# Mixture-of-experts outputs scaled and accumulated in DRAM instead of gathered back, in a decoder layer on one core

## The chip, the cores and the metric

The kernel is one launch on one core of a Trainium2 chip. The metric is the device time of that core in microseconds (us), the median of several executions. The engines are TensorE (PE, with its weight loads as PEld), VectorE (DVE), ScalarE (ACT), GpSimd (POOL) and SyncE (SP, which only issues transfers here). Sixteen DMA engines carry the transfers.

## The reference, cut to what matters

The layer works on 16 sequences of 256 tokens with 256 features each, 4096 tokens in all. It has three sublayers, each followed by a residual sum and a layer norm: gated linear attention, cross attention, and a mixture of 8 experts of which every token uses two. Only the third is touched:

```
probs = softmax(xf @ router_w.T)                 # 4096 x 8
topv, topi = top_k(probs, 2)
probs = probs * mask(topi);  probs /= probs.sum(-1) + 1e-9
g = einsum('nd,edf->nef', xf, gate_w) + gate_b   # d 256, f 512
u = einsum('nd,edf->nef', xf, up_w) + up_b
expert_out = einsum('nef,efd->ned', silu(g) * u, down_w) + down_b
y = einsum('ne,ned->nd', probs, expert_out)
out = layernorm(xf + y)
```

## The kernel before, in words

`decoder_layer` runs five stages one after the other. Each engine has its own instruction list in a stage, the lists are ordered among each other by semaphores only, and a stage begins when all engines and its transfers are through with the one before.

1. `linear_attention` and 2. `cross_attention` work sequence by sequence. The second ends a sequence by storing its normalised rows twice (`store_x2`, lines 888 to 891): into the SBUF tile `x2_all`, and into the DRAM tensor `x2_rows`. Its SP list begins with the loads of the first rows (lines 893 and 894).

3. `route_tokens` picks two experts for each token, almost all of it in one chain of small DVE instructions that each wait for the last (`link`, line 1484). It leaves the gates, the place (`slots`) of each of a token's two copies in a list sorted by expert, the same place as column and row, and a table that tells which expert a tile of the list belongs to.

4. `run_experts` inverts the places by one-hot matmuls into `token`, the token of each place, and then works through 23 tiles of the sorted list: 16 big ones of 512 rows and 7 half ones of 256. Products are made in three matmuls of high and low parts. For a tile t the lists interleave neighbouring tiles by hand:
   - PE: `gate_up` of t for f = 0 and 1, `down` of t-1 (one group of 12 matmuls for each 128 rows, alternating between two PSUM tiles `ps_y`, each of which must have been read by `keep_y` before it is used again, line 1955), `turn_x` of t+1, then `gate_up` for f = 2 and 3.
   - DVE: `hidden` 0 and 1, `keep_y` of t-1 (line 1854: PSUM plus bias into `y_out`), `hid_low` 0 and 1 (line 1880), `tile_index` of t+2 (line 1865), `x_low` of t+1, `hidden` and `hid_low` 2 and 3, `dn_low`.
   - ACT: `gu_high` of t+1, `gates` 0 and 1, `hid_high` 0 and 1, `x_high`, `dn_high`, `gates` and `hid_high` 2 and 3.
   - POOL: `low_parts` of t+1 (line 1767: four subtractions of 128x512 that make `gu_lo`), then `gather_rows` of t+2 (line 1758: one indirect transfer of 128 rows for each block, 4 or 2).
   - SP: weights of t+2, the store of y of t-1 into `y_sorted` (line 1719, after a wait for `keep_y`), biases of t+1.

5. `combine` takes the 32 blocks of 128 tokens in 16 groups of two. POOL gathers each token's two rows of `y_sorted` by `slots` (line 2023, 64 indirect transfers). DVE adds both, each times its gate, to `x2_all` (lines 2046 and 2052), takes mean and variance (lines 2057, 2061) and normalises (line 2067); ACT makes the root of the variance (lines 2034, 2036); SP stores (line 2090).

What orders the work around the change is thus POOL's list in stages 4 and 5, DVE's in stage 5, and the waits on `y_kept` and `y_stored`.

## Time and profile before

| | |
|---|---|
| time, median of 3 executions | 1540.83 us (1540.05 to 1543.04) |
| the profiled execution, its own time | 1540.89 us |
| its span, first to last instruction | 1539.0 us |
| mean granted TensorE clock | 0.927 |
| PE busy | 1315.0 us, 85% |
| DVE busy | 873.6 us, 57% |
| ACT busy | 890.7 us, 58% |
| POOL busy | 726.5 us, 47% |
| HBM read, written | 83.93 MB, 28.26 MB |

The busy shares are averages over five stages that have different limits, so what the change is worth has to be read stage by stage. All times in the rows are counted from the start of the span. By them cross attention runs from 747 us to about 1001, the routing to 1037, the experts to 1437, and the final stage to the end.

### The profile page before, as it was taken

To read this page: it belongs to the slowest core of one execution; us is meant where nothing else is said; L and a number is where in the kernel's file an instruction comes from. 1 tells how busy PE (TensorE), PEld (TensorE's weight loads), DVE (VectorE), ACT (ScalarE), POOL (GpSimd) and SP (SyncE) were. 2 spreads that over 40 slices of the span, in tenths; PEclk is the share of its full clock that TensorE was granted. 3 is DMA by queue.
4 is the path that set the end of the run, shared out by engine and by line. 5 is a ranking of instruction groups with operands and counts; after the bars stand their busy time and mean duration, and the time that the engine had idled before them with its cause. 6 is when DMAs were issued, how large, how long until landed. Compare 5 with 4: busy or idle time off the path is not lost. (4 is left out here: it accounts for less than half of the span.)

```text
span 1539.0 us, 31104 instructions
## 1 busy us (share of the span) xinstructions
PE 1315.0 (85%) x10439; PEld 1110.6 (72%) x10439; DVE 873.6 (57%) x1806; ACT 890.7 (58%) x2018; POOL 726.5 (47%) x861
## 2 busy tenths in 40 slices
PE   5899999999999999999689999804999999998200
PEld 4788888888888888887467777604788888898200
DVE  3345554544455545445378888577555555567447
ACT  4677777777777777777327777600554555455101
POOL 2244444444444444445347777402555454555464
PEclk9999999999999999999789999955899999999655
DMA  3300000000000000001123433204354545455244
GB/s 130 77 16 22 29 29 29 23 29 15 28 22 29 29 24 27 29 9 36 45 64 95 108 106 107 92 1 131 115 181 146 157 154 166 161 179 155 88 121 133
DMA packets 127907, 120.61 MB, mean 78 GB/s; under 512 B 42498, under 2 KB 108650, under 8 KB 127786
## 3 DMA queue, kind: packets, MB, share of 16 engines
q1 hardware_dynamic: 120970, 100.42, 21.0%
q0 software_dynamic: 6816, 18.62, 4.6%
q8 instruction: 70, 1.15, 0.3%
q14 instruction: 51, 0.42, 0.1%
HBM read 83.93 MB, written 28.26 MB: 73 GB/s over the span
## 5 line engine op out<-in xcount | busy, mean ns | idle before, releaser
L293 POOL TENSOR_SCALAR_AFFINE_SELECT a_decay<-a_decay 128x256 f32<-128x256 f32 x256 | 115.3, 454 | 258.7 <-ACT a_decay L373 257.2
L496 DVE TENSOR_TENSOR a_probs<-a_ps_s,a_decay 128x384 f32<-128x384 f32 x256 | 131.6, 552 | 158.3 <-PE a_ps_o L676 147.4
L302 POOL TENSOR_TENSOR a_key_sum<-a_probs 128x256 f32<-128x256 f32 x128 | 94.5, 738 | 170.0 <-DVE a_probs L496 158.0
L336 ACT ACTIVATE a_qk_exp<-a_ps_qk 128x512 f32<-128x512 f32 x128 | 76.5, 598 | 136.9 <-PE a_ps_qk L582 130.0
L1767 POOL TENSOR_TENSOR e_gu_lo<-e_gu_raw,e_gu_hi 128x512 fp32r<-128x512 f32 x92 | 117.3, 1305 | 72.2 <-ACT e_gu_hi L1788 72.2
L582 PE MATMUL a_ps_qk<-a_xT_hi,a_w_hi 128*128 128x256 f32 x512 | 145.0, 283 | 3.6 <-ACT a_qk_relu L337 3.6
L582 PE MATMUL a_ps_qk<-a_xT_hi,a_w_lo 128*128 128x256 f32 x512 | 143.9, 281 | 0.0
L582 PE MATMUL a_ps_qk<-a_xT_lo,a_w_hi 128*128 128x256 f32 x512 | 143.8, 281 | 0.0
L489 DVE SCALAR_TENSOR_TENSOR a_qk<-a_qk_exp,a_qk_relu 128x512 f32<-128x512 f32 x128 | 89.2, 697 | 96.1 <-ACT a_qk_relu L337 96.0
L657 PE MATMUL a_ps_s<-a_qk 64*128 64x256 f32 (+1 forms) x1024 | 131.7, 337 | 0.7 <-DVE a_probs L496 0.5
L1758 POOL DMA_INDIRECT e_x_in<-x_rows,e_index x78 | 75.0, 961 | 115.6 <-DVE e_index L1865 98.5
L371 ACT ACTIVATE a_decay<-a_ps_c,a_c_now 128x256 f32<-128x256 f32 x256 | 124.4, 486 | 1.8 <-PE a_ps_c L647 1.2
L1816 ACT CAST e_hid_hi<-e_hid 128x512 fp32r<-128x512 f32 (+1 forms) x92 | 48.9, 554 | 128.0 <-PE e_ps_y L1958 87.5
L670 PE MATMUL a_ps_o<-a_probs,a_values 128*64 128x256 f32 (+1 forms) x1024 | 111.5, 339 | 0.4 <-DVE a_probs L496 0.4
L657 PEld LDWEIGHTS a_ps_s<-a_qk 64*128 64x128 f32 x1024 | 107.3, 186 | 2.5 <-issue 2.5
L582 PEld LDWEIGHTS a_ps_qk<-a_xT_hi,a_w_hi 128*128 128x128 f32 x512 | 98.0, 191 | 5.8 <-issue 5.6
L373 ACT ACTIVATE a_decay<-a_ps_c,a_c_now 128x128 f32<-128x128 f32 x256 | 98.4, 384 | 0.0
L582 PEld LDWEIGHTS a_ps_qk<-a_xT_hi,a_w_lo 128*128 128x128 f32 x512 | 98.1, 192 | 0.0
L582 PEld LDWEIGHTS a_ps_qk<-a_xT_lo,a_w_hi 128*128 128x128 f32 x512 | 97.9, 191 | 0.1
L307 POOL TENSOR_TENSOR a_oT_lo<-a_oT,a_oT_hi 128x256 fp32r<-128x256 f32 x128 | 94.4, 737 | 1.2 <-ACT a_oT_hi L390 1.2
L1874 DVE SCALAR_TENSOR_TENSOR e_hid<-e_ps_u,e_bias,e_gate 128x512 f32<-128x512 f32 (+1 forms) x92 | 61.0, 668 | 57.3 <-ACT e_gate L1810 45.7
L955 POOL TENSOR_TENSOR b_probs<-b_probs,b_top 128x1232 f32<-128x1232 f32 x32 | 72.7, 2272 | 43.3 <-DVE b_top L1132 43.3
(282 smaller groups left out, 4007.7 us busy)
## 6 DMA issues: line engine op xcount, KB each, us to landing
e_gu_raw<-in_L_ffn_gate_w SPq DMA_DIRECT2D x23, 512.0 KB
e_gu_raw<-in_L_ffn_up_w SPq DMA_DIRECT2D x23, 512.0 KB
e_dn_raw<-in_L_ffn_down_w SPq DMA_DIRECT2D x23, 512.0 KB, 4.4
y_sorted<-e_y_out SPq DMA_DIRECT2D x16, 512.0 KB
a_x_in<-in_x SPq DMA_DIRECT2D x16, 256.0 KB, 2.8
a_x_res<-in_x SPq DMA_DIRECT2D x16, 256.0 KB, 2.8
x_rows<-a_x SPq DMA_DIRECT2D x16, 256.0 KB, 2.1
x_bo_rows<-a_x_bo SPq DMA_DIRECT2D x16, 256.0 KB, 2.1
```

Source lines behind the costliest of these rows:

```text
L293: pool.affine_select(out=d, in_=d, compare_op=ALU.is_ge, fill=0.0, base=0, pattern=[[0, 2], [1, P]], channel_multiplier=-1)\
L302: pool.tensor_tensor(key_sum[:], probs[:, :, P:N], probs[:, :, N:TRI], ALU.add).then_inc(keys_summed, 1)
L307: pool.tensor_tensor(oT_lo[g % 2][:], oT[g % 2][:], oT_hi[g % 2][:].bitcast(F32), ALU.subtract).then_inc(oT_lo_done, 1)
L336: act.activation(qk_exp[:], ps_qk[:], ACT.Exp)
L371: act.activation(decay[h][:, 0:N], ps_c[:, h, :], ACT.Exp, bias=c_now[:, 0, head:head + 1], scale=-1.0)
L373: act.activation(decay[h][:, N:TRI], ps_c[:, h, P:N], ACT.Exp, bias=c_now[:, 1, head:head + 1], scale=-1.0).then_inc(decay_exp[h], 1)
L489: vec.scalar_tensor_tensor(qk[g][:], qk_exp[:], 1.0, qk_relu[:], ALU.min, ALU.add).then_inc(qk_done, 1)
L496: vec.tensor_tensor(probs[:, h, :], ps_s[h][:, 0:TRI], decay[h][:], ALU.mult)\
L582: mm = pe.matmul(out, l, r, start=(n == 0), stop=(n == len(todo) - 1))
L657: mm = pe.matmul(ps_s[h][:, out], qk[g][rows, 1, j], qk[g][rows, 0, i], start=True, stop=True)
L670: pe.matmul(out[h][:, 0, cols], values[par][:, j, 2 * g + h, :], probs[:, h, keys], start=(j == 0), stop=(j == 1), skip_group_check=True)
L1767: ins = pool.tensor_tensor(gu_lo[par][:, k, cols], gu_raw[par][:, k, cols], gu_hi[par][:, k, cols].bitcast(F32), ALU.subtract)
```

## The change

- A token's rows in DRAM get four more columns (`META`), written by the routing: the difference of the two gates, the second gate, the number of the first expert, the first gate. The gather of a tile brings them along, and DVE works out from them each row's `share`, the gate that belongs to this tile's expert.
- ACT multiplies the rows of `y_out` by their share. POOL adds them by indirect accumulating transfers to the tokens' rows of a new DRAM tensor `sum_rows`, in which cross attention has put the rows themselves. Those of tile t are issued when the ones of tile t-1 have landed.
- Places that no token uses get targets of their own (`spare`, 512 more rows, zeroed at the start of cross attention).
- `x2_all`, `slots`, `y_sorted` and the store of y are gone. The final stage loads `sum_rows` in order, in 8 groups of four blocks, and shares out the normalising: two blocks to ACT, one to DVE, one to POOL.

```diff
 def cross_attention(...):
+        spare = sb("b_spare", [P, D + META])
             def store_x2(b):
                 sp.wait_ge(x2_ready, b + 1)
-                sp.dma_start(x2_all[:, bass.ts(b, NB), :], x2[:]).then_inc(x2_stored, 16)
+                sp.dma_start(sum_rows[b], x2[:]).then_inc(x2_stored, 16)
                 sp.dma_start(x2_rows[b], x2[:]).then_inc(x2_stored, 16)
 
+            sp.wait_ge(spare_ready, 1)
+            for n in range(B * N, x2_dram.shape[0], P):
+                sp.dma_start(x2_dram[n:n + P, :], spare[:]).then_inc(spare_stored, 16)
+                sp.dma_start(sum_dram[n:n + P, :], spare[:, 0:D]).then_inc(spare_stored, 16)
             sp.dma_start(x_in[:], x1_rows[0]).then_inc(x_in_loaded, 16)
...
         def _(pool):
+            pool.memset(spare[:], 0.0).then_inc(spare_ready, 1)
...
 def route_tokens(...):
+        @block.sync
+        def _(sp):
+            sp.wait_ge(meta_ready, 1)
+            sp.dma_start(x2_dram[0:plan.TOKENS, D:D + META].rearrange("(n p) m -> p n m", p=P), meta[:]).then_inc(meta_stored, 16)
+            sp.wait_ge(meta_stored, 16)
...
                 if k == 0:
+                    link(vec.tensor_scalar(meta[:, :, 2], col[:], -1.0, float(E), ALU.mult, ALU.add))
...
                 link(vec.tensor_tensor(gates[k][:], top[k][:], rcol[:], ALU.mult))
+            link(vec.tensor_tensor(meta[:, :, 0], gates[0][:], gates[1][:], ALU.subtract))
+            link(vec.tensor_copy(meta[:, :, 3], gates[0][:]))
+            vec.tensor_copy(meta[:, :, 1], gates[1][:]).then_inc(meta_ready, 1)
...
-                vec.tensor_copy(slots[k][:], slot_f[:]).then_inc(slots_ready, 1)
-                vec.wait_ge(slots_ready, k + 1)
...
 def run_experts(...):
-            def load_biases(e, par):
+            def load_biases(e, t, par):
+                if has(t, -2):
+                    for n in range(2):
+                        sp.wait_ge(y_kept[n], rounds(t - 1))
...
-                if has(t, -1):
-                    store(t - 1, 1 - par)
...
+            pool.iota(spare_i[:], pattern=[[0, -(-COLS // TB)], [P, TB]], base=plan.TOKENS + 1, channel_multiplier=1).then_inc(counts_ready, 1)
...
+            def add_rows(t, par, turn):
+                pool.wait_ge(y_scaled, first_block(t + 1))
+                pool.wait_ge(target_ready, t + 1)
+                if has(t, -1):
+                    pool.wait_ge(y_stored[1 - par], 16 * plan.blocks_of_parity(t - 1, turn - 1 + par))
+                pool.sem_inc(pool_turns, 1)
+                for blk in range(blocks(t)):
+                    pool.indirect_dma_start(sum_dram, bass.IndirectOffsetOnAxis(target[par][:, blk:blk + 1], 0),
+                                            y_out[par][:, blk, :], None, compute_op=ALU.add).then_inc(y_stored[par], 16)
+
             def tile(t, par, turn):
                 if has(t, 1):
                     low_parts(1 - par, turn + par)
+                if has(t, -1):
+                    add_rows(t - 1, 1 - par, turn - 1 + par)
                 if has(t, 2):
                     gather_rows(t + 2, par, turn + 1)
...
+                def scale_y(blk):
+                    act.wait_ge(y_kept[blk % 2], rounds(t - 1) + blk // 2 + 1)
+                    act.activation(y_out[1 - par][:, blk, :], y_out[1 - par][:, blk, :], ACT.Copy,
+                                   scale=share[1 - par][:, blk:blk + 1]).then_inc(y_scaled, 1)
+
                 gates(0)
                 gates(1)
+                if has(t, -1):
+                    act.wait_ge(share_ready, t)
+                    for blk in range(blocks(t - 1) - 1):
+                        scale_y(blk)
                 hid_high(0)
                 hid_high(1)
+                if has(t, -1):
+                    scale_y(blocks(t - 1) - 1)
...
             def keep_y(t, par, turn):
-                vec.wait_ge(y_stored[par], 16 * turn)
+                if has(t, -2):
+                    vec.wait_ge(y_stored[par], 16 * plan.blocks_of_parity(t - 2, turn - 1))
+                vec.tensor_copy(target[par][:, 0:blocks(t)], token[:, bass.ds(first_block(t), blocks(t))]).then_inc(target_ready, 1)
...
+            def shares(t, par):
+                if has(t, -2):
+                    vec.wait_ge(y_scaled, first_block(t - 1))
+                nb = blocks(t)
+                vec.scalar_tensor_tensor(share[par][:, 0:nb], x_in[par][:, 0:nb, D + 2], expert_of[:, bass.ds(t, 1)],
+                                         x_in[par][:, 0:nb, D], ALU.is_equal, ALU.mult).then_inc(share_step, 1)
+                vec.wait_ge(share_step, t + 1)
+                vec.tensor_tensor(share[par][:, 0:nb], share[par][:, 0:nb], x_in[par][:, 0:nb, D + 1], ALU.add).then_inc(share_ready, 1)
...
                     x_low(t + 1, 1 - par)
+                    shares(t + 1, 1 - par)
...
-            vec.tensor_copy(token[:], ps_u[0][:, 0:COLS]).then_inc(token_kept, 1)
+            vec.scalar_tensor_tensor(used[:], ps_u[0][:, 0:COLS], 0.0, spare[:, 0:COLS], ALU.is_equal, ALU.mult).then_inc(token_kept, 1)
             vec.wait_ge(token_kept, 1)
+            vec.scalar_tensor_tensor(token[:], ps_u[0][:, 0:COLS], -1.0, used[:], ALU.add, ALU.add).then_inc(token_kept, 1)
...
 def combine(...):
-    G = 2
-    BUFS = 4
+    G = 4
+    ON_ACT = (0, 1)
+    ON_VEC, ON_POOL = 2, 3
...
+            for i in range(GROUPS):
+                sp.dma_start(rows[i][:], sum_rows[:, cols(i), :]).then_inc(loaded[i], 16)
+            for i in range(GROUPS):
+                sp.wait_ge(act_done, i + 1)
+                sp.wait_ge(vec_done, i + 1)
+                sp.wait_ge(pool_done, i + 1)
+                sp.dma_start(out_rows[:, cols(i), :], rows[i][:]).then_inc(stored, 16)
...
+            def statistics(i):
+                vec.wait_ge(loaded[i], 16)
+                for j in range(G):
+                    vec.bn_stats(stats[:, i * G + j, :], rows[i][:, j, :]).then_inc(counted, 1)
+                vec.wait_ge(counted, G * (i + 1))
+                vec.sem_inc(vec_turns, 1)
+                for j in range(G):
+                    ins = vec.bn_aggr(mv[:, i * G + j, :], stats[:, i * G + j, :])
+                ins.then_inc(var_ready, 1)
+
+            def normalise(i):
+                vec.wait_ge(rstd_ready, i + 1)
+                vec.scalar_tensor_tensor(shift[:, cols(i)], mv[:, cols(i), 0], -1.0, rstd[:, cols(i)], ALU.mult, ALU.mult)\
+                    .then_inc(shift_ready, 1)
+                n = i * G + ON_VEC
+                vec.tensor_scalar(rows[i][:, ON_VEC, :], rows[i][:, ON_VEC, :], mv[:, n, 0:1], rstd[:, n:n + 1],
+                                  ALU.subtract, ALU.mult).then_inc(vec_done, 1)
```

In the new final stage DVE and ACT each do the first step of group i and then the normalising of group i-1, and POOL normalises its block of group i.

## Rows read from the trace of the kernel before

**Rows 1.** Windows: stretch, length, PE PEld DVE ACT POOL busy (count), PEclk, DMA share, GB/s.

```profile
1200.00:1240.00 40.00, 40.00 (x235) 35.14 (x234) 23.02 (x36) 21.08 (x29) 20.21 (x19) 1.00 0.56 174
...
1437.00:1539.00 102.00, 0.00 (x0) 0.00 (x0) 56.21 (x160) 9.28 (x33) 62.26 (x65) 0.51 0.41 124
...
1049.00:1051.00 2.00, 0.17 (x1) 0.02 (x1) 2.00 (x3) 1.04 (x1) 2.00 (x2) 0.50 1.01 374
```

**Rows 2.** Groups by line, 1430 to 1539: count, busy us, mean ns, idle before, releaser.

```profile
L2023 POOL DMA_INDIRECT f_y<-y_sorted,slots x64 | 62.2, 971 | 25.9 <-issue 19.2 <-DVE f_stats L2057 6.7
...
L2057 DVE BATCH_NORM_STATS2 f_stats<-f_resid 128x6 f32<-128x256 f32 x32 | 12.0, 419 | 3.0 <-DVE f_resid L2052 2.6
L2067 DVE TENSOR_SCALAR f_resid<-f_resid,f_mv,f_rstd 128x256 f32<-128x256 f32 x32 | 11.8, 410 | 0.0
L2034 ACT ACTIVATE f_ln_var<-f_mv,f_eps_col 128x2 f32<-128x2 f32 x16 | 4.7, 296 | 88.3 <-DVE f_mv L2061 54.0 <-issue 21.6 <-remote 12.8
L2061 DVE BATCH_NORM_AGGREGATE f_mv<-f_stats 128x2 f32<-128x6 f32 x32 | 4.0, 166 | 4.3 <-issue 1.7 <-DVE f_stats L2057 1.7
```

**Rows 3.** Chain that ended last, final stage: start, length, what.

```profile
1457.51 2.63 DMA f_y<-y_sorted,slots
```

**Rows 4.** Timeline, both ends of the final stage: start, length, engine, line, operation, idle before.

```profile
1434.34 0.43 DVE L1854 TENSOR_TENSOR e_y_out<-e_ps_y,e_dn_bias 128x256 f32<-128x256 f32 x1 [2.07 <-PE e_ps_y L1958]
...
1437.35 0.10 POOL L2015 MEMSET f_eps_col<- 128x1 f32 x1 [19.55 <-POOLq L1617]
...
1534.77 1.42 DVE L2067 TENSOR_SCALAR f_resid<-f_resid,f_mv,f_rstd 128x256 f32<-128x256 f32 x4
```

**Rows 5.** Page, part 6, transfers: count, KB each, median us to landing.

```profile
e_dn_raw<-in_L_ffn_down_w SPq DMA_DIRECT2D x23, 512.0 KB, 4.4
...
a_x_in<-in_x SPq DMA_DIRECT2D x16, 256.0 KB, 2.8
```

**Rows 6.** Timeline of a big tile, 1220 to 1239: POOL, then ACT, then DVE.

```profile
1221.05 5.05 POOL L1767 TENSOR_TENSOR e_gu_lo<-e_gu_raw,e_gu_hi 128x512 fp32r<-128x512 f32 x4 [2.87 <-ACT e_gu_hi L1788]
1230.79 0.97 POOL L1758 DMA_INDIRECT e_x_in<-x_rows,e_index  x1 [4.69 <-DVE e_index L1865]
...
1238.37 5.07 POOL L1767 TENSOR_TENSOR e_gu_lo<-e_gu_raw,e_gu_hi 128x512 fp32r<-128x512 f32 x4 [2.86 <-ACT e_gu_hi L1788]
...
1227.95 1.15 ACT L1816 CAST e_hid_hi<-e_hid 128x512 fp32r<-128x512 f32 x2 [4.83 <-PE e_ps_y L1958]
...
1223.82 0.42 DVE L1854 TENSOR_TENSOR e_y_out<-e_ps_y,e_dn_bias 128x256 f32<-128x256 f32 x1
...
1228.61 1.29 DVE L1880 TENSOR_TENSOR e_hid_lo<-e_hid,e_hid_hi 128x512 fp32r<-128x512 f32 x2 [0.29 <-ACT e_hid_hi L1816]
1229.82 0.16 DVE L1865 CAST e_index<-e_token 128x4 uint32 x1
```

**Rows 7.** Timeline of a half tile, 1370 to 1382: POOL, then DVE.

```profile
1370.91 5.23 POOL L1767 TENSOR_TENSOR e_gu_lo<-e_gu_raw,e_gu_hi 128x512 fp32r<-128x512 f32 x4 [2.56 <-ACT e_gu_hi L1788]
...
1381.32 5.24 POOL L1767 TENSOR_TENSOR e_gu_lo<-e_gu_raw,e_gu_hi 128x512 fp32r<-128x512 f32 x4 [1.79 <-ACT e_gu_hi L1788]
...
1373.62 2.81 DVE L1880 TENSOR_TENSOR e_hid_lo<-e_hid,e_hid_hi 128x256 fp32r<-128x256 f32 x2
```

**Rows 8.** Timeline, start of the experts: DVE without and with POOL's subtractions beside it.

```profile
1045.26 1.93 DVE L1911 TENSOR_SCALAR e_col_hot<-e_count,slot_col,e_number 128x78 fp32r<-128x78 f32 x8
...
1048.24 5.85 DVE L1911 TENSOR_SCALAR e_col_hot<-e_count,slot_col,e_number 128x78 fp32r<-128x78 f32 x8
...
1048.88 4.93 POOL L1767 TENSOR_TENSOR e_gu_lo<-e_gu_raw,e_gu_hi 128x512 fp32r<-128x512 f32 x4 [11.11 <-ACT e_gu_hi L1788]
```

**Rows 9.** Timeline of cross attention: its start (SP, PE), and ACT's normalising near its end.

```profile
747.37 0.38 SPq L893 DMA_DIRECT2D b_x_in<-x_rows  x1
...
753.08 1.09 PE L1237 MATMUL b_ps_m<-ident,b_x_in 128*128 128x128 f32 x4 [0.24 <-ACT b_rwT L987]
...
996.34 1.09 ACT L1041 ACTIVATE b_x<-b_resid,b_shift,b_rstd 128x256 f32<-128x256 f32 x2
```

More of the change, by code:

```diff
@@ L16 @@
 LN_EPS = 1e-5
+META = 4
 class Shapes:
@@ L1837, in _ @@
             all_tiles(act, tile)
+            last = TILES - 1
+            act.wait_ge(share_ready, TILES)
+            for blk in range(blocks(last)):
+                act.wait_ge(y_kept[blk % 2], rounds(last) + blk // 2 + 1)
+                act.activation(y_out[last % 2][:, blk, :], y_out[last % 2][:, blk, :], ACT.Copy,
+                               scale=share[last % 2][:, blk:blk + 1]).then_inc(y_scaled, 1)
         @block.vector
@@ L1919, in _ @@
             x_low(0, 0)
+            shares(0, 0)
             dn_low(0, 0)
@@ L2005, in combine @@
[L2005 to L2009 removed]
+        rows = [sb(f"f_rows{i}", [P, G, D]) for i in range(GROUPS)]
+        stats, mv = sb("f_stats", [P, NBK, 6]), sb("f_mv", [P, NBK, 2])
@@ new lines, in _ @@
+        @block.vector
+        def _(vec):
+            def statistics(i):
[14 more added lines that the diff above has]
+                                  ALU.subtract, ALU.mult).then_inc(vec_done, 1)
+            for i in range(GROUPS):
+                statistics(i)
+                if i:
+                    normalise(i - 1)
+            normalise(GROUPS - 1)
@@ L2085, in _ @@
[L2085 to L2092 removed]
+                n = i * G + ON_POOL
+                pool.wait_ge(rstd_ready, i + 1)
```

183 lines of the change are left out of this document (71 added, 112 removed).

## The prediction

> **What bounds the kernel now.** I read the windows by stage first, then the groups by line of the final stage and its chain, then the timelines of one big and one half tile. In a window of big tiles PE is busy all 40.00 us of 40, at the full clock, POOL half of them, the DMA engines 0.56 [rows 1]: PE bounds the big tiles, and what is added to other engines there is free until it makes PE wait. In the final stage PE does nothing, and POOL is the busiest with 62.26 of 102 us [rows 1]. Its 64 gathers take 62.2 us, with 25.9 us of idle time before them, 19.2 of it the gaps of 0.3 us between two issues [rows 2]; the chain goes gather, landing (2.63 us from an issue), DVE [rows 3]. So the stage is set by one gather after the other at 0.97 + 0.30 = 1.27 us, 81 us in all, and the rest is DVE's sums. It runs from 1437.35 to 1539.0 [rows 4], 101.7 us, 6.6% of the span. This is what the change can win.
>
> **The final stage, after.** No gathers; 8 loads and 8 stores of 512 KB. DVE has for each group four statistics at 12.0/32 = 0.375 us (1.50), four aggregates at 4.0/32 = 0.125 (0.50), one block normalised at 11.8/32 = 0.37, all [rows 2], a small operation for the shift (0.2, the nearest is the index copy of 0.16 [rows 6]) and two waits on its own semaphores, 0.1 each: 2.8 us, 22.4 for eight. ACT has a root (two operations of at most 0.30 [rows 2]) and two blocks of 1.09 together [rows 9], 1.7 us a group, less than DVE. The first load lands in 4.4 us [rows 5]. Behind the last statistics come root 0.6, shift 0.2, ACT's blocks 1.1, waits 0.3 and a store of 4.4, less the 0.6 of DVE's own last step that is counted already. Sum: 4.4 + 22.4 + 6.0 = 32.8, say 33 us.
>
> The transfers are the unknown. 512 KB land 1.6 us later than 256 KB [rows 5], which by itself would mean 3.2 us for each further 512 KB, and 4.4 + 15 x 3.2 = 52 us for loads and stores in a row. With the DMA engines full, 374 GB/s are moved [rows 1], 1.4 us for 512 KB, 22 us for all 16. Eight loads queued at once are the second case, so I take the 33 of DVE. Bounds 30 and 52. The term is 33 - 101.7 = **-68.7 us** (-72 to -50).
>
> **The seam before it.** Now y is kept at 1434.77 and the stage begins at 1437.35 [rows 4]. After: ACT's scaling 0.6, POOL's lead before a run of indirect transfers 0.8 (the index copy ends at 1229.98, the gather starts at 1230.79 [rows 6]), a second issue 1.27 later, landing 2.63 [rows 3]: 1440.1. An accumulating transfer is not in this trace; its landing is bounded by that of a gather from below and, with no row near, by twice that from above; I add 0.4. **+3 us** (2.5 to 6).
>
> **Big tiles.** A tile is 1238.37 - 1221.05 = 17.3 us [rows 6]. POOL's list becomes subtraction, adds, gathers: 5.05 + 0.2, then twice a lead of 0.8 and 5.0 for four issues = 16.9 us. That fits by 0.4. In time: ACT is through with `hid_high` at 1229.1 [rows 6], the last scaling at 1229.6 (0.5, half of the 1.09 [rows 9]; the three before it lie in ACT's 4.83 us of idle time [rows 6]), adds 1230.4 to 1235.4, gathers 1236.2 to 1241.2. The subtraction that began at 1238.37 now runs from 1241.3 to 1246.4; PE needs it only in the next tile. The 0.5 us on ACT before `x_high`, the two `shares` operations and the target copy on DVE have slack in the tile, since PE is fed two halves ahead. One thing I don't take as free. The target copy stands in front of `keep_y`, which starts at 1223.82, one period later 1241.15, next to the new start of the subtraction. Of what DVE does beside a subtraction the trace shows this: eight `col_hot` operations take 1.93 us, and 5.85 us with a subtraction beside them [rows 8]; two `hid_low` take 2.81 us beside one in a half tile [rows 7] and 1.29 us for twice the columns without [rows 6]. Each seems to wait for one of the four subtractions, 5.05/4 = 1.26 us. A copy held so long delays the reading of a PSUM tile that PE wants back one group of 12 matmuls later, 2 us or less by 235 matmuls in 40 us [rows 1], of which reading itself needs 0.42 [rows 6]. So between 0 and 1.3 us for each of 15 tiles; I take 0.33. **+5 us** (0 to 19).
>
> The Trainium skill says in "SBUF — State Buffer", section "Who interferes with whom", that copies and casts in a two-port mode share a port pair with GpSimd, and that the one issued second is blocked until the other is through. The rows on `col_hot` agree; that a copy of four elements is held too, no row here shows. By the rule alone the term would be that of the rival below.
>
> **Half tiles.** The period is 1381.32 - 1370.91 = 10.4 us [rows 7], already a loop of POOL's 5.2 us and the DVE work that waits for its end. POOL's list becomes 5.24 + 0.2 + 2 x (0.8 + 0.97 + 0.3 + 0.95) = 11.5 us, 1.1 more, in the five half tiles that have all three jobs; and `shares` adds 0.4 us to the loop of DVE. The larger counts: **+5 us** (0 to 10).
>
> **Small edits.** Cross attention: SP must wait for POOL's memset (0.3) and issue eight spare stores at 0.4 each before the first load, which now goes at 747.37 [rows 9]; it goes at about 751.2 and lands in 2.8 us [rows 5] or a little more behind 1 MB of stores: 754.5, where PE wanted it at 753.08 [rows 9]. **+1.5 us** (0 to 4). `x2_all` becomes a store to DRAM, with the same count of issues at the same places of SP's list; nothing. Routing: four small DVE operations in, two out; three of the new ones fall where DVE waits for PE; nothing. The store of 16-byte pieces has the rest of the routing, some 24 us from the gates to its end, as cover; without it, it would delay the first gather. Start of the experts: three small DVE operations more, **+0.6**. SP loses 23 stores and keeps the same waits before the biases. The new wait of the adds is for those of the tile before, issued 17 us (10 in half tiles) earlier; behind it stand POOL's gathers and subtraction, and it stays empty unless four adds take that long.
>
> **The sum**: -68.7 + 3 + 5 + 5 + 1.5 + 0.6 = -53.6, a span of 1485.4. The profiled execution took 1540.89 for a span of 1539.0, 1.9 more, and lies 0.06 above the median; so the median is 1487.
>
> **Rivals.**
> - *Issuing an add costs more than a gather.* With I for an issue and its gap, each 1 us above 1.27 costs 4 us in a big tile, less the 0.4 of slack, and 2 in a half one: 74 (I - 1.27) - 6 on top, and less for small ones. At one and a half times (0.97 becomes 1.45) that is 29 us, 1516. For: it writes by address to DRAM and must read as well. Against: all 64 gathers stay close to 0.97, whatever else goes on. Chance 0.12.
> - *The same, and slower than before.* The place is POOL's list in the experts. It decides from I = 1.27 + 60/74 = 2.1 us; at 3 us the time would be 1487 + 122 = 1609. The same is reached where the four adds of a tile take over 17.3 + 3.4 us to land, 5 us each, against 2.63 for a gather. Chance 0.06. "Collectives: The Full Stack" of the Trainium skill, section "The bandwidth ceiling", says that an add in the DMA engines needs two reads where a copy needs one and runs at half its rate; no row here shows one. That would be 128 KB more in each, far from 5 us, and it leaves the chance small.
> - *The target copy always waits for a whole subtraction.* 15 x 1.3 instead of 5: 1501. For: the new start of the subtraction and the copy fall together. Against: the subtraction may fall just behind, and PE has about a microsecond of slack. Chance 0.10.
> - *The final stage is bounded by transfers*, 52 us for 33: 1506. Chance 0.08.
> - *All additions hide*: without the two terms of 5 and the 1.5, 1475. Chance 0.04. That the change doesn't do what it says can't be more than part of this: 64 gathers leave the final stage in any case.
> - The forecast: 0.60, own range 1479 to 1495.
>
> **Range and chances.** 1476 to 1517 leaves out the slower case, the best one, and half of the dear issue, some 0.16 to 0.2. A difference of 0.2% (3 us) is about what can be told from none. Faster by more: all but the slower case and what lies beside it, 0.93; the same 0.01; slower 0.06.
>
> **What would show it.** The final stage should be 30 to 36 us with DVE busy nearly throughout and no wait for a load after the first; if DVE waits for loads, that term is wrong. The group of adds on POOL should show 0.95 to 1.0 us each; if 1.4 or more, the first rival. PE should stay at 40 of 40 in big tiles, at a period of 17.3 to 17.7; if PE waits on DVE's `keep_y` there, the copy is held. The half tiles should have a period near 11.4 and POOL with hardly a gap. The first PE work on x in cross attention should come 1 to 2 us late. A chain that goes through the landing of adds before the last tile would prove me wrong altogether.

## The result, and the profile after

The changed kernel takes 1508.97 us (1504.07 to 1511.16, four runs) beside 1541.30 (1540.05 to 1543.04) for the kernel before: a ratio of 0.9777, with a 95% interval of 0.976 to 0.9793. The forecast was 1487, the range 1476 to 1517. So the direction and the range held, and of the 54 us that were expected about 32 came.

The profiled execution took 1509.18 us for a span of 1507.5, against 1539.0 before. I cut both spans at the same two events on VectorE: the first operation of the experts' stage (the copy that makes `e_count`) and the start of the last kept y rows. The times are starts in the timelines.

| stretch, us | before | after | difference | forecast |
|---|---|---|---|---|
| to the start of the experts | 1037.8 | 1040.7 | +2.9 | +1.5 |
| from there to the first tile index of the loop | 54.2 | 54.4 | +0.2 | +0.6 |
| 14 periods of big tiles | 241.8 | 250.5 | +8.7 | +5 |
| last big one and the half tiles, six periods | 73.8 | 94.4 | +20.6 | +5, with the next line |
| to the last kept y | 26.8 | 29.9 | +3.2 | |
| seam and final stage | 104.7 | 37.6 | -67.1 | -65.7 |

The end came out as forecast; the loss is in the middle, above all in the half tiles. First the windows, with the columns of [rows 1]:

```profile
1200.00:1240.00 40.00, 39.95 (x228) 34.66 (x227) 28.11 (x45) 24.27 (x38) 34.88 (x28) 1.00 0.59 142
1360.00:1400.00 40.00, 31.99 (x210) 30.12 (x211) 19.96 (x45) 20.55 (x39) 28.25 (x22) 0.88 0.55 130
1400.00:1440.00 40.00, 34.00 (x248) 33.53 (x246) 26.91 (x51) 23.16 (x44) 31.00 (x25) 0.87 0.59 166
1480.00:1507.00 27.00, 0.00 (x0) 0.00 (x0) 16.75 (x80) 12.95 (x33) 9.88 (x8) 0.50 0.89 312
```

In the big tiles PE still looks fully busy, 39.95 of 40 [rows 1]. It is not as productive: 228 matmuls in the window against 235. A busy share near its limit hides a period that has grown from 17.33 to 17.86 us. POOL went from 20.21 to 34.88 busy, and with the gaps of 0.3 us between issues that is all of its time. In the half tiles PE is down to 32 and 34 of 40, and its granted clock to 0.88 and 0.87. In the kernel before, the clock of the window from 1360 to 1400 was 1.00.

Why POOL is full, by its groups over the experts' stage (busy us, mean ns, idle time before and what ended it):

```profile
L1796 POOL DMA_INDIRECT sum_rows<-e_y_out,e_target x78 | 126.6, 1623 | 45.9 <-ACT e_y_out L1851 21.2 <-issue 19.9 <-ACT e_y_out L1884 4.5
L1785 POOL TENSOR_TENSOR e_gu_lo<-e_gu_raw,e_gu_hi 128x512 fp32r<-128x512 f32 x92 | 116.6, 1304 | 20.2 <-ACT e_gu_hi L1819 19.9
L1776 POOL DMA_INDIRECT e_x_in<-x_rows,e_index x78 | 79.7, 1022 | 45.4 <-DVE e_index L1926 22.2 <-issue 21.9 <-DMA sum_rows<-e_y_out,e_target 0.9
```

An add takes POOL 1.62 us to issue, a gather 1.02 beside it and 0.97 in [rows 2]. I had costed the adds at the gather's price. The timeline of one big tile, POOL's list and then two operations of VectorE in the same tile (start, length):

```profile
1214.44 5.06 POOL L1785 TENSOR_TENSOR e_gu_lo<-e_gu_raw,e_gu_hi 128x512 fp32r<-128x512 f32 x4
1219.67 1.88 POOL L1796 DMA_INDIRECT sum_rows<-e_y_out,e_target  x1 [0.17 <-issue]
1221.86 1.56 POOL L1796 DMA_INDIRECT sum_rows<-e_y_out,e_target  x1 [0.30 <-issue]
...
1227.41 1.09 POOL L1776 DMA_INDIRECT e_x_in<-x_rows,e_index  x1 [0.30 <-issue]
...
1232.32 1.31 POOL L1785 TENSOR_TENSOR e_gu_lo<-e_gu_raw,e_gu_hi 128x512 fp32r<-128x512 f32 x1
...
1217.46 3.20 DVE L1941 TENSOR_TENSOR e_hid_lo<-e_hid,e_hid_hi 128x512 fp32r<-128x512 f32 x2 [0.28 <-ACT e_hid_hi L1847]
1220.59 0.42 DVE L1926 CAST e_index<-e_token 128x4 uint32 x1
```

No wait for another engine stands in POOL's list ("issue" is time in which it waited for nothing that the profile shows): it ends at 1232.3 and starts again at once, 17.88 us after 1214.44. Beside it two `hid_lo` take 3.20 us instead of 1.29 [rows 6]: VectorE's work has come to lie beside POOL's subtraction.

The half tiles open with a stall, in the last big tile. The timeline again, VectorE, POOL, TensorE:

```profile
1355.26 5.14 DVE L1900 CAST e_target<-e_token 128x4 uint32<-128x4 f32 x1
...
1355.43 4.94 POOL L1785 TENSOR_TENSOR e_gu_lo<-e_gu_raw,e_gu_hi 128x512 fp32r<-128x512 f32 x4
1368.69 1.62 POOL L1796 DMA_INDIRECT sum_rows<-e_y_out,e_target  x1 [8.33 <-ACT e_y_out L1851]
...
1376.17 1.00 POOL L1776 DMA_INDIRECT e_x_in<-x_rows,e_index  x1 [0.30 <-ACT e_gu_hi L1819]
...
1397.89 1.11 PE L2001 MATMUL e_ps_x<-ident,e_x_in 128*128 128x128 f32 x4 [6.15 <-DMA e_x_in<-x_rows,e_index]
```

A copy of four elements a row takes 5.14 us, to within 0.03 us of the end of POOL's subtraction. It comes to lie there because POOL's list has just become shorter: the first half tile has two gathers and not four, and so this subtraction begins 15.93 us after the one before it (1339.50) and not 17.86. The y rows behind the copy are kept late, so scaled late, so POOL waits 8.33 us before its adds, and the gathers stand behind the adds. What PE then waited for, from 1355 to 1470 (us, times, longest):

```profile
PE e_ps_x L2001 <- DMA e_x_in<-x_rows,e_index: 12.4, 4, 6.2
PE e_ps_g L2012 <- DVE e_hid L1935: 5.3, 4, 2.0
PE e_ps_y L2024 <- DVE e_y_out L1904: 4.1, 1, 4.1
PE e_ps_y L2024 <- DVE e_hid_lo L1941: 2.2, 1, 2.2
```

These waits are not the whole loss. The stretch from the start of the six periods to the last kept y, before and after, in the columns of [rows 1]; then two windows of the changed kernel in it:

```profile
1333.80:1434.34 100.54, 91.37 (x696) 86.81 (x694) 66.29 (x121) 53.39 (x98) 49.69 (x42) 0.99 0.50 154
1345.62:1469.91 124.29, 100.15 (x688) 95.23 (x687) 77.36 (x146) 62.69 (x117) 89.50 (x66) 0.90 0.52 125
1415.00:1420.00 5.00, 5.00 (x44) 5.00 (x44) 3.53 (x8) 3.41 (x6) 4.38 (x4) 1.00 0.88 236
1425.00:1430.00 5.00, 5.00 (x24) 5.00 (x25) 2.08 (x8) 2.38 (x5) 4.19 (x3) 0.50 0.56 137
```

PE sits idle 24.1 us instead of 9.2, which is 15.0 of the 23.8 us. The other 8.8 us are busy time: the same work takes 100.2 us instead of 91.4, and the granted clock of the stretch is 0.90 instead of 0.99. Between the two small windows PE was busy 0.55 of 5 us; behind that wait the clock stood at 0.50 of its full 2.4 GHz, and PE, busy all the time, started 24 matmuls where it had started 44. The matmuls of y follow each other every 0.21 us at 1361, at half the clock, and every 0.12 at 1211, at the full one.

The seam and the start of the final stage, then three pieces of the chain in one of its groups:

```profile
1470.37 0.51 ACT L1884 ACTIVATE e_y_out<-e_y_out,e_share 128x256 f32<-128x256 f32 x1 [0.87 <-DVE e_y_out L1904]
1471.70 1.54 POOL L1796 DMA_INDIRECT sum_rows<-e_y_out,e_target  x1 [4.54 <-ACT e_y_out L1884]
1473.55 1.54 POOL L1796 DMA_INDIRECT sum_rows<-e_y_out,e_target  x1 [0.30 <-issue]
1479.76 7.38 SPq L2083 DMA_DIRECT2D f_rows<-sum_rows  x8
```

```profile
1486.20 1.30 DVE f_stats L2096 x4
...
1487.63 0.38 DVE f_mv L2100 x4
...
1488.06 0.38 DVE f_rows L2108
```

The final stage runs from 1479.76 to 1507.5, 27.8 us where it took 101.7 [rows 4]. Its chain is VectorE's from the first load's landing at 1484.24 on: 2.21 us a group, with no wait for a load after the first.

### The profile page after: what moved, and what is told of

The parts are those of the page before. It is cut to its first block and busy times, and to the rows that moved or that the text cites. A ratio compares the mean times of both kernels' runs of the same rounds, so it can differ in the third digit from the quotient of the medians.

```text
span 1507.5 us, 31113 instructions
## 1 busy us (share of the span) xinstructions
PE 1331.5 (88%) x10439; PEld 1124.8 (75%) x10439; DVE 873.7 (58%) x1799; ACT 930.7 (62%) x2096; POOL 804.1 (53%) x885
## 3 DMA queue, kind: packets, MB, share of 16 engines
q0 software_dynamic: 14976, 20.62, 7.5%
## 5 line engine op out<-in xcount | busy, mean ns | idle before, releaser
L1796 POOL DMA_INDIRECT sum_rows<-e_y_out,e_target x78 | 126.6, 1623 | 45.9 <-ACT e_y_out L1851 21.2
L490 DVE SCALAR_TENSOR_TENSOR a_qk<-a_qk_exp,a_qk_relu 128x512 f32<-128x512 f32 x128 | 89.1, 696 | 94.5 <-ACT a_qk_relu L338 94.4
L1785 POOL TENSOR_TENSOR e_gu_lo<-e_gu_raw,e_gu_hi 128x512 fp32r<-128x512 f32 x92 | 116.6, 1304 | 20.2 <-ACT e_gu_hi L1819 19.9
L1941 DVE TENSOR_TENSOR e_hid_lo<-e_hid,e_hid_hi 128x512 fp32r<-128x512 f32 (+1 forms) x92 | 91.2, 1010 | 33.4 <-ACT e_hid_hi L1847 32.3
L1776 POOL DMA_INDIRECT e_x_in<-x_rows,e_index x78 | 79.7, 1022 | 45.4 <-DVE e_index L1926 22.2
L2024 PE MATMUL e_ps_y<-e_dn_hi,e_hid_hi 128*128 128x256 f32 x312 | 89.9, 288 | 6.7 <-DVE e_y_out L1904 4.5
## 6 DMA issues: line engine op xcount, KB each, us to landing
a_x_in<-in_x SPq DMA_DIRECT2D x16, 256.0 KB
a_x_res<-in_x SPq DMA_DIRECT2D x16, 256.0 KB, 2.7
x_rows<-a_x SPq DMA_DIRECT2D x16, 256.0 KB, 2.2
x_bo_rows<-a_x_bo SPq DMA_DIRECT2D x16, 256.0 KB, 2.2
b_x_in<-x_rows SPq DMA_DIRECT2D x16, 256.0 KB, 3.0
```

Source lines behind the costliest of these rows:

```text
L1785: ins = pool.tensor_tensor(gu_lo[par][:, k, cols], gu_raw[par][:, k, cols], gu_hi[par][:, k, cols].bitcast(F32), ALU.subtract)
L1796: pool.indirect_dma_start(sum_dram, bass.IndirectOffsetOnAxis(target[par][:, blk:blk + 1], 0), y_out[par][:, blk, :], None, compute_op=ALU ...
L1941: vec.tensor_tensor(hid_lo[:, f, 0:rows], hid[n][:, 0:rows], hid_hi[:, f, 0:rows].bitcast(F32), ALU.subtract)\
L2024: mm = pe.matmul(ps_y[n][:, 0:D], h[:, f, rows], w[par][:, f, :], start=(s == 0), stop=(s == len(todo) - 1))
```

## The experiments

Absolute times of different comparisons stand on different chips: the kernel before took 1541 and 1545 us on two of them and 1529 to 1531 on three others. I could not place that difference; its mean granted clock was 0.928 to 0.931 where it took 1529 to 1532 us and 0.923 to 0.929 where it took 1543 to 1548, and which of the two made the other is not shown. In the kernels after the change the stretches agree from chip to chip: last kept y to end takes 37.6 and 37.3 us in the changed kernel on two chips, and 36.8 and 37.0 in e7 and e9, again on two. So between comparisons I go by stretches of the traces, and use ratios to tell how each kernel stands to the one before.

| run | ratio to before | big tile, us | 14 periods | six periods | start of experts to last y | to the end |
|---|---|---|---|---|---|---|
| before | 1 | 17.33 | 241.8 | 73.8 | 396.5 | 104.7 |
| changed | 0.9777 | 17.86 | 250.5 | 94.4 | 429.2 | 37.6 |
| e1 | 1.0321 | 23.87 | 323.4 | 91.5 | 501.1 | 36.4 |
| e2 | 1.0061 | 20.2 | 279.5 | 92.5 | 459.0 | 37.5 |
| e3 | 0.9782 | 17.5, 17.8 | 248.1 | 86.7 | 418.8 | 37.0 |
| e4 | 0.9932 | 18.3 | 256.1 | 96.1 | 435.8 | 37.5 |
| e5 | 0.9774 | 17.8, 18.8 | 254.1 | 94.3 | 432.8 | 37.3 |
| e6 | 0.9732 | 18.3 | 256.0 | 84.7 | 421.9 | 36.8 |
| e7 | 0.9696 | 18.1 | 253.9 | 80.9 | 417.5 | 36.8 |
| e8 | 0.9825 | 18.1 to 21.4 | 270.5 | 86.8 | 439.2 | 36.0 |
| e9 | 0.9684 | 17.53 | 246.3 | 73.7 | 402.1 | 37.0 |
| e10 | 0.9645 | 17.53 | 246.3 | 73.7 | 401.9 | 35.3 |
| e11 | 0.9680 | 17.85 | 249.0 | 76.0 | 407.5 | 31.3 |
| e12 | 0.9638 | 17.53 | 246.3 | 73.7 | 400.4 | 35.5 |

e1 to e4 shared a chip, e5 to e8 another, e9 to e11 a third; e12 ran on a fourth.

### e1: scatter instead of add

```
-  y_out[par][:, blk, :], None, compute_op=ALU.add)
+  y_out[par][:, blk, :], None)
```

> The indirect transfers of the experts' rows write them instead of adding them (the sums lose the tokens' own rows and one of the two experts); waits, lists and sizes stay. Theory A (the price of an add's issue on POOL, 1.62 us in the trace after against 1.02 for a gather, makes POOL the bound of the experts' stage): the issue falls to about 1.0, POOL's list of a big tile from 17.9 to 15.5 us, the period of a big tile returns to 17.3 (-8 us over 14 tiles), the half tiles lose 1.2 us of POOL each (-8): about 1492, 1485 to 1498. Rival B (the accumulating packets, 72 us of 16 engines, crowd the gathers and loads): the issue stays near 1.6 and the time falls all the same, by 10 or more, while the packets get shorter. Rival D (1.6 us is the price of any indirect destination): issue stays at 1.6, packets shorter or not, time within 3 us of 1509.

It became slower, 1579.32 us, ratio 1.0321 (1.0304 to 1.0339), where the cheaper issue was to make it faster. The price itself came out as expected. POOL's group, then the two operations that explain the rest, from the timelines:

```profile
L1796 POOL DMA_INDIRECT sum_rows<-e_y_out,e_target x78 | 80.6, 1033 | 163.1 <-ACT e_y_out L1851 140.0
```

```profile
1218.84 4.96 POOL L1785 TENSOR_TENSOR e_gu_lo<-e_gu_raw,e_gu_hi 128x512 fp32r<-128x512 f32 x4
...
1219.45 4.38 DVE L1900 CAST e_target<-e_token 128x4 uint32 x1
```

An issue costs 1.03 us without the addition and 1.62 with it: 0.59 us is the addition's, not the scatter's, which rules out rival D. But POOL's shorter list moved the subtraction against VectorE's: the target copy now begins 0.61 us after the subtraction, as it does in most big tiles, and ends with it, at 1223.83 against 1223.80. The 23 copies take 73.9 us in all, against 10.0 in the changed kernel, and the period is 23.87. So a cheaper step made the kernel some 5% slower, by its phase. As a test of what the add's price costs it failed; e11 had to do that. Nor can it decide on rival B, since the held copies set its pace. The packets did change: the same 20.62 MB move in half of them and half the time, as the page's rows of the software queue show (packets, MB, share of 16 engines; the changed kernel, then e1). What speaks against rival B is e9, which has all 14,976 packets of the adds and yet a period of 17.53 us.

```profile
q0 software_dynamic: 14976, 20.62, 7.5%
```

```profile
q0 software_dynamic: 7488, 20.62, 3.8%
```

### e2: gathers ahead of adds

```
 if has(t, 1): low_parts(...)
+if has(t, 2): gather_rows(t + 2, ...)
 if has(t, -1): add_rows(t - 1, ...)
-if has(t, 2): gather_rows(t + 2, ...)
```

> On POOL the gather of tile t+2 is issued before the adds of tile t-1. Theory A: the list of a big tile keeps its length, 17.9 us; what goes is the stall in which the gathers of the half tiles stood behind adds that waited for the scaled rows and a landing (PE waited 12.4 us for x rows between 1360 and 1460): half tiles fall from 13.7 to 11 or 12 us; about 1492, 1484 to 1500. Rival E (POOL now waits for the index, which VectorE has only 8.8 us after the tile begins, with the adds behind it): idle of up to 3.8 us a big tile, period 18.5 to 21, time 1515 to 1560.

1539.34 us, ratio 1.0061 (1.0044 to 1.0077). Rival E's number held, 20.2 us a big tile, but not quite for its reason:

```profile
1207.48 5.59 POOL L1785 TENSOR_TENSOR e_gu_lo<-e_gu_raw,e_gu_hi 128x512 fp32r<-128x512 f32 x4
1215.20 1.01 POOL L1776 DMA_INDIRECT e_x_in<-x_rows,e_index  x1 [2.13 <-DVE e_index L1926]
...
1210.27 3.96 DVE L1941 TENSOR_TENSOR e_hid_lo<-e_hid,e_hid_hi 128x512 fp32r<-128x512 f32 x2 [0.28 <-ACT e_hid_hi L1847]
```

POOL waits 2.13 us for the index, and the index is late because it stands behind two `hid_lo` of 3.96 us (5.55 in the next tile) instead of 1.29, beside POOL's subtraction. The subtraction holds up the copy for which POOL then waits. The half tiles gained nothing: 92.5 for 94.4 in the six periods, and 2.5 us more from there to the last kept y. Theory A's 1492 failed.

### e3: half of the subtraction on VectorE

```
-for k in range(KC):      # POOL
+for k in range(1, KC):
+vec.tensor_tensor(gu_lo[par][:, 0, :], gu_raw[par][:, 0, :],
+                  gu_hi[par][:, 0, :]..., ALU.subtract)
```

> Half of the gate and up weights' subtraction (two of POOL's four of 1.30 us) goes to VectorE as one of 128x1024, about 1.1 us, while it waits for the turned rows. Theory A: POOL's list of a big tile is 17.9 - 2.6 = 15.3 us, under PE's 17.33, so the period returns to 17.3 to 17.4 (-8 us) and the half tiles gain up to 2.6 each (-10): 1491, 1484 to 1500. Rival B (transfers) or rival C (VectorE and its chain with ScalarE are what slows the tile): no gain, within 3 us of 1509, or slower by up to 1.1 us a tile, 1509 to 1534.

1497.17 us, ratio 0.9782 (0.9766 to 0.9799). By the ratio nothing was gained, but that chip ran the kernel before in 1529.46. By the stretches it gained 2.4 us in the big tiles (expected 8) and 7.7 in the half tiles (expected 10), and its span is 10.3 us shorter than that of the changed kernel. The 2.4 us are no more than one kernel shows by itself (e5); what tells is that the single periods alternate between 17.5 and 17.8, where they were 17.8 to 17.9. The theory of POOL's list as the only bound is too simple for the big tiles.

### e4: one more memset on POOL

```
+pool.memset(pad[par][:], 0.0)   # 128x512, in each tile
 for k in range(KC): ...         # the subtraction
```

> One more memset of 128x512 on POOL per tile, about 0.5 us (1.16 for 128x1280), used by nothing. Theory A: POOL's list bounds the big tiles, so each gains all of it: 0.5 x 15 = 8 us, and the half tiles 3: 1520, 1516 to 1523. Rival B or C: POOL has slack, the time stays within 2 us of 1509.

The memset takes 0.54 us. The big tiles went from 17.86 to 18.3, nearly all of them alike, +5.7 over 14 periods, and the next six +1.7. So 0.41 of the 0.54 us arrives in a period on average: POOL's list is at its limit. The span, 1515.0, is 7.5 above that of the changed kernel. The median of 1518.63 lies in the expected range.

### e5: the changed kernel again

> The changed kernel once more, unaltered, as the yardstick for the runs beside it: ratio 0.9777 within its interval (0.976 to 0.979), periods of the big tiles 17.8 to 17.9 us.

1511.16 us, ratio 0.9774 (0.9751 to 0.9797). Four of its 14 periods were 18.8 instead of 17.8, and the profile's span is 1.8 us longer; so differences of 4 us in that column are within what one kernel shows.

### e6: all of the subtraction on VectorE

```
-low_parts(1 - par, turn + par)          # POOL
 vec.tensor_copy(index[par]...)
+gu_low(0, ...)                          # VectorE, 128x1024
 x_low(t + 1, ...); shares(t + 1, ...)
+gu_low(1, ...)
```

> All of the gate and up weights' subtraction goes to VectorE (two of 128x1024, 1.22 us each), so that POOL issues transfers and nothing else; the order of its list stays. Theory F (the shared access: VectorE's copies and its subtractions of two SBUF operands stand still while POOL's subtraction runs, and POOL's list of 17.9 us is the bound): nothing is held, hid_lo back to 0.65 us each, the target copy 0.16 us always, the big tiles' period 17.33; the half tiles keep the loop of add, gather and turned rows, 12 to 14 us: 12 to 22 us less than the changed kernel beside it. Rival (VectorE and ScalarE are the bound, or the adding packets): the same as the changed kernel or slower, by up to 2.4 us a tile, 55 us.

1503.81 us, ratio 0.9732 (0.9714 to 0.975), 7.4 us less than the run beside it where 12 to 22 were expected. Nothing is held any more: the target copies take 4.3 us in all. The half tiles gained 9.7 us. The big ones gained nothing, at 18.3 us; e7 shows the larger part of why.

### e7: the same, with the gathers first

> As the run before, and the gather of tile t+2 goes ahead of the adds of tile t-1. Theory F: the 43 us that this order cost beside POOL's subtraction came from its phase (hid_lo held 4 to 5.5 us, so the index late), so that without it the order costs nothing in the big tiles (17.33) and takes the half tiles from 13 or 14 us to 10.4 to 11.5: 20 to 35 us less than the changed kernel, around 0.96 of before. Rival (the order itself costs, since POOL waits for the index): periods above 18 again, slower than the run before.

The edit is e6's with e2's. 1498.8 us, ratio 0.9696 (0.9677 to 0.9714). The order that cost 30 us in the experts' stage beside POOL's subtraction (e2: 459.0 for 429.2) now saves 4.4 (417.5 for 421.9): it was the subtraction beside it that cost, not the order. The gain is smaller than expected, 12.4 us below the changed kernel beside it. The reason stands in one timeline:

```profile
1206.44 1.22 DVE L1898 TENSOR_TENSOR e_gu_lo<-e_gu_raw,e_gu_hi 128x1024 fp32r<-128x1024 f32 x1
...
1207.58 0.74 DVE L1930 SCALAR_TENSOR_TENSOR e_hid<-e_ps_u,e_bias,e_gate 128x512 f32<-128x512 f32 x1
...
1208.38 0.50 PE L2011 MATMUL e_ps_g<-e_xT_hi,e_gu_hi 128*128 128x512 f32 x1 [0.29 <-DVE e_hid L1930]
```

The second piece stands ahead of `e_hid` on VectorE, and PE waits for that, some 0.3 us a tile, and its weight loads 0.7. It was the place I had chosen for it; e9 puts the pieces elsewhere and has 17.53 us for these 18.1.

### e8: no addition, and the target copy on ScalarE

```
-vec.tensor_copy(target[par]..., token[...])
+act.copy(target[par]..., token[...])    # and e1's edit
```

> The scatter without addition again (the sums lose the tokens' own rows and one of the two experts), with the copy of the targets on ScalarE instead of VectorE. Theory F: its 23.7 us a big tile came from this copy of 4 elements a row, which stood 4.4 us behind POOL's subtraction with PE behind it; on ScalarE it takes 0.2 us, the period falls to 17.4 or less and the time from 1579 to between 1475 and 1490. Rival (plain scatters land late, or something else in that phase): the period stays above 20 us.

1517.12 us, ratio 0.9825 (0.98 to 0.9851), against 1.0321 for e1 (on different chips, so with care). The periods of 23.87 fall to 19.2 in most tiles, by about the 4.4 us of the held copy, and the experts' stage from 501.1 to 439.2. Beside e1 only the copy was moved, so its place was what cost there. The period did not fall to the 17.4 that I expected. POOL waits 4.1 to 4.8 us in most tiles for the scaled rows, and ScalarE up to 3.8 before `e_gate` for something that the trace does not name. What holds this kernel at 19 is open.

### e9: the subtraction in VectorE's gaps

```
 for blk in range(blocks(t)):            # keep_y
     vec.tensor_tensor(y_out[par][:, blk, :], ps_y..., dn_bias..., ALU.add)
+    if blk < blocks(t) - 1:
+        gu_low(PIECES[blk:blk + 1], ...)    # 128x512
```

> As e7 (all subtraction on VectorE, gathers first), with the subtraction in four pieces of 128x512 of about 0.65 us: three of them between the blocks of the kept y rows, where VectorE sat idle 1.0 us each time, the last behind the index. Theory: e7's 18.1 us a big tile is 17.33 plus a wait of TensorE for e_hid, which stood behind the second piece of 1.22 us on VectorE; out of the way, the period returns to 17.3 or 17.4 (-10 us) and the half tiles from 12 to 11 (-5): ratio to before 0.957 to 0.963. Rival (TensorE's own work or transfers set the 18.1): ratio 0.968 to 0.971 again.

1481.86 us, ratio 0.9684 (0.9669 to 0.9699). The trace did what was expected: 17.53 us a big tile (of 17.3 or 17.4), and the half tiles in 73.7 us, those of the kernel before. The ratio did not follow: 0.9684 lies where the rival had it (0.968 to 0.971) and not at 0.957 to 0.963. But there the kernel before took 1530.22, and against e7's 1498.8 the time is 17 us less, the span 18.7. It is the period, not the ratio, that decides here. The window and the place where the pieces went:

```profile
1200.00:1240.00 40.00, 40.00 (x231) 35.39 (x230) 27.77 (x51) 24.09 (x37) 25.02 (x20) 1.00 0.65 166
```

```profile
1210.55 0.42 DVE L1905 TENSOR_TENSOR e_y_out<-e_ps_y,e_dn_bias 128x256 f32<-128x256 f32 x1 [0.40 <-PE e_ps_y L2032]
1210.89 0.68 DVE L1893 TENSOR_TENSOR e_gu_lo<-e_gu_raw,e_gu_hi 128x512 fp32r<-128x512 f32 x1
```

VectorE still waits 0.40 us for each y: the 0.68 fit into a gap of 1.0. The 0.2 us that are left over the old period lie in the matmuls of y: from the first of them to the first that turns x it is 5.75 us (1207.48 to 1213.23), where it was 5.46 before (1204.90 to 1210.36). Why is not shown.

### e10: all the mends

```
 sp.dma_start(x_in...); sp.dma_start(x_bo...)
+for n in ...: the eight spare stores
...
 for blk in range(blocks(last)):         # the last tile's adds
+    pool.wait_ge(y_scaled, first_block(last) + blk + 1)
     pool.indirect_dma_start(...)
```

> As e9, with two more: the eight stores of the spare rows behind the first loads of cross attention instead of ahead of them (theory: the late start is what brought the experts' stage 3 us later; 1.5 to 3 us back), and the last tile's adds issued block by block, each behind its own scaled rows (about 1 us of the seam of 9.4). Together 2.5 to 4 us less than e9: ratio 0.955 to 0.961. Rival: the 3 us belong to the longer stores of the tokens' rows and to other work, nothing comes back.

1475.93 us, ratio 0.9645 (0.9632 to 0.9658). The start of the experts came 3.0 us earlier than in e9 (1036.35 for 1039.38), the end stretch was 1.6 us shorter: 4.7 together and 5.9 by the medians, where 2.5 to 4 were expected. The ratio expected, 0.955 to 0.961, was missed for the same reason as in e9. The load of x is issued at once instead of at 751.15, behind eight stores:

```profile
745.94 0.38 SPq L897 DMA_DIRECT2D b_x_in<-x_rows  x1
...
751.64 1.09 PE L1247 MATMUL b_ps_m<-ident,b_x_in 128*128 128x128 f32 x4 [0.24 <-ACT b_rwT L997]
```

In the changed kernel that work of PE starts at 754.12, after 1.74 us of waiting for the load.

### e11: scaled rows stored in order

```
-add_rows(t - 1, ...)                    # POOL, all tiles
+sp.wait_ge(y_scaled, first_block(t + 1))
+sp.dma_start(y_sorted[...], y_out[par]...)
```

> The changed kernel with its scaled rows stored in order by one transfer of SyncE a tile, as before the change, in place of POOL's adds (the experts' part is missing from the output); scaling, shares, target copies and the final stage stay. Theory (all that the experts' stage lost hangs on the adds): periods 17.3 in the big tiles and 10.4 to 10.8 in the half tiles, seam 3 to 4 us; 35 to 42 us less than the changed kernel, ratio 0.950 to 0.956. Rival (the scaling, the shares, the bias loads behind the kept rows, or the copies cost a part): ratio 0.96 or more.

1481.18 us, ratio 0.968 (0.9665 to 0.9695); the experts' stage is 21.7 us shorter than in the changed kernel and the end 6.3, 28 in all where 35 to 42 were expected. The ratio lies in the rival's range. The half tiles are nearly whole again, 76.0 us. The big tiles are not, 17.85, although POOL now waits for the index and for `e_gu_hi` in each. Half a microsecond a tile has nothing to do with adds:

```profile
1212.42 1.12 DVE L1896 CAST e_target<-e_token 128x4 uint32 x1
1213.46 0.87 DVE L1900 TENSOR_TENSOR e_y_out<-e_ps_y,e_dn_bias 128x256 f32<-128x256 f32 x2
```

The copy waits again, beside the subtraction of 1209.72 to 1214.76, and gets in ahead of its end, about where the third of the four operations ends (1209.72 + 3 x 1.26 = 1213.5). It does so in all 15 big tiles, 1.10 to 1.12 us each. That this is the half microsecond can be seen on PE: from the first matmul of y to the first that turns x it takes 6.08 us here (1210.83 to 1216.91) and 5.75 in e9, where the copy is free, and that is the whole difference between their periods (17.85 and 17.53).

### e12: e10 again

> The kernel of e10 once more, to see what its ratio owes to the chip: the kernel before took 1529 to 1530 us in two of the comparisons and 1541 to 1545 in the others, while traces of kernels after the change agree step by step. If only the kernel before differs between the chips, this one takes 1473 to 1478 us again wherever it runs, and its ratio is 0.955 where before takes 1545 and 0.9645 where it takes 1530. If the whole chip is slower, it takes 1487 to 1491 beside 1545, ratio 0.9645 again.

1474.14 us, ratio 0.9638 (0.9625 to 0.9651), on a chip where the kernel before took 1530.76. So it repeats e10, but did not meet a chip with 1541 or more, and the question that it was for stays open.

## Why the prediction was right and wrong

**The final stage: right in kind, too dear by 5 us.** It is VectorE's chain and not the transfers', so the rival of 1506 falls. The load landed in 4.48 us (4.4 said). A group took 2.21 us (2.8 said): statistics 1.30 to 1.33 for 1.50, aggregates 0.38 for 0.50, and shift and waits 0.2 for 0.4. Term: -73.9 for -68.7.

**The seam: +6.8 for +3.** From the end of the last kept y (1470.33) it takes 9.4 us, before it took 2.6. Scaling and POOL's lead of 0.8 were sized well. The second issue came 1.85 us after the first, for 1.27. The failed piece is the landing: from the second issue's start to the next stage 6.2 us, where I had a gather's 2.63 and 0.4. e11 without adds is 6.3 us shorter at the end, and e10 won 1.6 by splitting the wait.

**The big tiles: +8.7 for +5, by another mechanism.** The step that failed is "four issues at a gather's 1.27 with its gap". Four adds take from 1219.67 to 1227.11, 7.4 us. The first rival put a price on it: with an issue and gap of 1.92 it gives 74 x 0.65 - 6 = 42 us on top, 1529, and it came to 1509. It was too dear because the same sum held two leads of 0.8 that are gaps of 0.17 and 0.30 once POOL is never waiting. So the list is 17.88, not 16.9 + 4 x 0.65 = 19.5. e4 shows that this list bounds: a memset of 0.54 us a tile brought 0.41. And e11 shows that there is a second limit at almost the same height, PE's own work with the held copy in it, 17.85 with no add at all. Taking one away wins next to nothing; that is why e3 and e6 disappointed in the big tiles. Only e9 (and e10 and e12, which contain it), with neither and with VectorE's order kept, got to 17.53.

**The half tiles: +23.8 for +5. This is where most of the missing 22 us are.** The list that I summed to 11.5 us was about right: it takes 11.2 (subtraction at 1393.89 to the end of the last gather at 1405.07) to 12.5, since the leads that never came pay for the dearer adds. What failed is the step from it to "1.1 more, in the five half tiles", as if the list only had to be gone through. The six periods took 22.5, 15.9, 8.9, 19.9, 12.6 and 14.6 us where they had been 17.3, 14.0, 11.2 and three of 10.4. POOL's list closes a loop there: gathers stand behind adds, adds behind scaled rows, these behind kept rows and the target copy, and that copy behind POOL's own subtraction. With half a tile of matmuls as cover the loop reaches PE, 12.4 us of waiting for gathered rows. On top of it comes a cost for which the sum had no term at all: behind these waits the granted clock falls to its lower level, and of the 23.8 us 8.8 are matmuls that took longer. So a wait of PE was worth more here than its own length. Where PE waits less the clock stays up: 0.98 over the same stretch in e9 and in e11, with 93.6 and 93.9 us busy. Each link of the loop shows in a run: no adds, 76.0 us (e11); no subtraction on POOL, 84.7 (e6); and gathers first as well, 80.9 (e7); the pieces out of VectorE's way, 73.7, with all adds in place (e9). So the adds themselves needn't cost these six periods anything; in this order, beside that subtraction, they do. (The piece from there to the last kept y stays longer in e9, 29.7 us for 26.8.)

**The target copy.** It was my third rival at 0.10, as "always waits", 1501. In the changed kernel it hardly waits in the big tiles (0.16 us in most, 10.0 us in 23), but once it waits for 5.14 us, and that is at the entry to the half tiles. I had sized the longest wait at one operation of the four, 1.26 us, and the bound of the term with it. The size was wrong: 4.38 us in e1 and 5.14 here (5.16 in e5), until the last of the four was through. This is the other step that failed. The Trainium skill has the rule in "SBUF — State Buffer", section "Who interferes with whom": copies and casts can take the port pair that they share with GpSimd, and an instruction of two SBUF inputs meets GpSimd's reads; whoever comes second is blocked. The held copies and the held `hid_lo` agree with it that there is a block; on who is blocked, one row doesn't agree: the copy at 1355.26 was recorded 0.17 us ahead of POOL's subtraction (POOL's times are rough) and was held all the same. `e_hid`, which reads PSUM, took 0.75 us beside the subtraction in the kernel before and in e1, as it did without. How many instructions of GpSimd in a row a blocked one waits for differs in these rows, up to four in e1 and what is left of one in e11, and what decides it is open.

**The start: +2.9 for +1.5.** All of it is the spare stores. Counted from the last store of linear attention (at 744.07 before, 743.53 in the changed kernel, 742.54 in e10) the experts begin 293.7, 297.2 and 293.8 us later: the stores ahead of the loads cost 3.5 us, and e10 has them all back. PE waited 1.74 us for the load, so the stage lost more than the first wait of PE that I had counted; where the rest arose is not shown.

**What I said would show it.** "If 1.4 or more, the first rival": it was 1.62, and the first rival's mechanism is what happened. "The half tiles should have a period near 11.4": they had 8.9 to 19.9. Those two were the right places to look.

**The range.** That 1509 lies within 1476 to 1517 is partly luck. Three of the six terms came out beyond their own bounds: the half tiles at 23.8 for 10 at most, the seam at 6.8 for 6, the final stage at -73.9 for -72. The room up to 1517 was made for other things, a dear issue above all, and the half tiles used it.

**What remains.** e10 and e12 keep the change and win its losses back: 1476 and 1474 us, spans of 1473.6 and 1472.3 for 1507.5, and ratios of 0.9645 and 0.9638 where the changed kernel has 0.9777 (that one measured on chips where the kernel before was slower, so that the ratios, if they err, understate what the mends won). They show that the forecast's 1487 was within reach, though not with the change's order of work and with the subtraction on POOL.

## What to carry to other kernels

Sum a queue's list with measured prices for each kind of entry, and where one kind is not in the trace, ask for the price at which that queue becomes the bound; then look for loops through it, since a list that fits by its sum can still hold up what stands behind its waits. A wait of TensorE that the sum finds can also cost more than its length, by the clock behind it. When work is added to GpSimd, look up which of VectorE's small copies and two-operand subtractions can come to lie beside its tensor operations: what they cost depends on the phase, so that a faster step (e1) or a better order (e2) can make the kernel slower. What helped here, in both orders tried (e6, e7), was to take the tensor work off GpSimd; it helped most in gaps of VectorE that the timeline shows, in pieces smaller than the gap (e9).

## What the runs showed of the hardware that I had not expected

- The issue of an indirect transfer with addition takes GpSimd 1.62 us in the mean of 78, mostly 1.54 to 1.57 and 1.62 to 1.88 for the first of a row; without addition 1.03. The addition also doubles the packets for the same 20.62 MB, 14,976 for 7,488, and their share of the DMA engines, 7.5% for 3.8%.
- A VectorE copy of four elements a row took up to 5.14 us, until the last of four GpSimd subtractions that followed each other was through, and 5.61 in e4, where a memset stood ahead of the four; free of them it takes 0.16, so its cost is all phase.
- Waits of TensorE in the half tiles, 15.0 us more than before, came with 8.8 us of slower matmuls, at a granted clock of 0.90 over the stretch for 0.99.
- The stage after the last adds began 4.7 us after the end of their issue, which waits for their landing, where a gather's landing took 2.63 us from its issue on [rows 3].
- The kernel before differs by 1% between chips (1529 to 1545 us), while the changed kernels' stretches agree within a few tenths of a per cent. A ratio from one chip may not be held against one from another.
